# The first slice of a weight load moved from SyncE's DMA queue to ScalarE's, ahead of the edge lists

## The reference, cut to what matters

```python
h = maximum(layernorm(x), 0)                      # x: 1024 x 512, float32
q = h @ Wq + bq;  k = h @ Wk + bk;  v = h @ Wv + bv
adj = zeros(1024, 1024).at[src, dst].set(1)       # 33792 edges
a = q @ k.T / sqrt(512) * adj + (1 - adj) * (-1e6)
x = x + softmax(a) @ v
h = maximum(layernorm(x), 0)
agg = segment_sum(h[src], dst) / max(deg, 1)[:, None]
return x + h + alpha * (agg @ W.T + b)
```

## Time and profile before

| | |
|---|---|
| median of 3 runs | 245.27 us |
| the three runs | 243.74, 245.29, 245.27 us |
| the profiled execution's own time | 245.4 us |
| its span | 243.6 us |
| mean granted TensorE clock over the span | 0.993 |
| PE busy | 235.3 us (97%) |
| DVE busy | 167.7 us (69%) |
| ACT, POOL busy | 81.5 us (33%), 69.9 us (29%) |
| HBM read, written | 7.09 MB, 2.10 MB |

### The profile page before, as it was taken

How to read it: one execution, slowest core, us unless ns; L and a number is a source line. 1 busy time by engine, 2 the same in 40 slices (tenths; PEclk the granted TensorE clock), 3 DMA queues, 4 the chain that set the end, 5 groups by cost and what they waited for, 6 DMA issues and landing times.

```text
span 243.6 us, 3378 instructions
## 1 busy us (share of the span) xinstructions
PE 235.3 (97%) x1296; PEld 189.4 (78%) x1296; DVE 167.7 (69%) x348; ACT 81.5 (33%) x147; POOL 69.9 (29%) x104
## 2 busy tenths in 40 slices
PE   7999898999999996999999999999999999999995
PEld 4356687887888885888888888888888888888885
DVE  6989998999999951588457997666656254054222
ACT  2399858523322211143062425142421102050000
POOL 4155452000000005994160546162334404100000
PEclk9999999999999997999999999999999999999999
DMA  6990000000020001004000000000000000001232
GB/s 198 337 364 12 1 0 3 0 0 3 0 47 0 0 3 43 1 3 174 0 0 0 3 0 0 0 3 0 0 0 3 0 0 1 3 3 43 86 116 99
DMA packets 5617, 9.42 MB, mean 39 GB/s; under 512 B 864, under 2 KB 1376, under 8 KB 5600
## 3 DMA queue, kind: packets, MB, share of 16 engines
q1 hardware_dynamic: 4880, 8.91, 10.5%
q10 hardware_dynamic: 720, 0.28, 0.4%
HBM read 7.09 MB, written 2.10 MB: 38 GB/s over the span
## 4 chain that ended last, share of the span: by engine, by line
PE 90%; ACT 3%; DVE 2%; POOL 2%; DMA 2%; issue 1%; ACTq 0%; DVEq 0%
PE bank L799 21%; PE bank L801 20%; PE bank L800 20%; PE bank L948 12%; PE bank L820 7%; PE bank L874 3%; PE bank L968 3%; DMA src_i<-in_src 2%; PE bank L867 1%; PE bank L859 1%; POOL var_e L352 1%; POOL rstd L347 1%; ACT h L419 1%; ACT h L432 1%; ACT A L447 0%
## 5 line engine op out<-in xcount | busy, mean ns | idle before, releaser
L550 DVE TENSOR_TENSOR ohW<-iotaW,key_b 128x640 bf16<-128x640 bf16 (+4 forms) x66 | 29.8, 452 | 0.0
L546 DVE TENSOR_TENSOR ohL<-iotaL,lo_b 128x512 bf16<-128x512 bf16 x66 | 27.4, 415 | 1.8 <-PE bank L820 1.8
L799 PE MATMUL bank<-hT_hi,GT_hi 128*128 128x512 f32 x64 | 25.8, 404 | 1.9 <-DVE V_lo L642 1.9
L801 PE MATMUL bank<-hT_hi,GT_lo 128*128 128x512 f32 x64 | 25.6, 400 | 0.0
L800 PE MATMUL bank<-hT_lo,GT_hi 128*128 128x512 f32 x64 | 25.5, 399 | 0.0
L799 PE MATMUL bank<-V_hi,pT_hi 128*128 128x512 f32 x64 | 25.5, 399 | 0.0
L419 ACT ACTIVATE h2f<-xs,nmr,rstd 128x512 f32<-128x512 f32 x8 | 6.5, 817 | 56.1 <-POOL nmr L361 56.1
L800 PE MATMUL bank<-V_lo,pT_hi 128*128 128x512 f32 x64 | 24.9, 390 | 0.0
L801 PE MATMUL bank<-V_hi,pT_lo 128*128 128x512 f32 x64 | 24.9, 390 | 0.0
L948 PE MATMUL bank<-A,h_hi 128*128 128x512 f32 x64 | 24.9, 389 | 0.0
L948 PE MATMUL bank<-A,h_lo 128*128 128x512 f32 x64 | 24.9, 389 | 0.0
(11 more groups left out here) (135 smaller groups left out, 527.2 us busy)
## 6 DMA issues: line engine op xcount, KB each, us to landing
xs<-in_x SPq DMA_DIRECT2D x4, 512.0 KB, 8.8
out_dram<-o_sb SPq DMA_DIRECT2D x7, 256.0 KB, 2.0
wq_raw<-in_wqT SPq DMA_DIRECT2D x4, 256.0 KB, 6.3
wk_raw<-in_wkT SPq DMA_DIRECT2D x4, 256.0 KB, 6.9
wv_raw<-in_wv SPq DMA_DIRECT2D x1, 1024.0 KB, 12.0
wt_raw<-in_wT SPq DMA_DIRECT2D x1, 1024.0 KB, 5.4
bv_sb<-in_bv SPq DMA_DIRECT2D x1, 256.0 KB, 3.3
b_sb<-in_b SPq DMA_DIRECT2D x1, 256.0 KB, 3.2
```

Of the source, the lines that this page charges most:

```text
L546: nc.vector.tensor_tensor(ohL[:, q % RING, :, :].rearrange("p b (m two) -> p b m two", two=2), bcast(iotaL[:, :].rearrange("p (m two) -> p ...
L550: nc.vector.tensor_tensor(ohW[:, q % RING, :, 0:row].rearrange("p b (m two) -> p b m two", two=2), bcast(iotaW[:, 0:row].rearrange("p (m t ...
L799: mm(out, lhs[0][a], rhs[0][b], start=(first and k == 0), stop=False)
L801: last = mm(out, lhs[1][a], rhs[0][b], start=False, stop=(final and k == len(pairs) - 1))
```

## The change

The load of slice 0 of wk leaves SP's list, where it stood second, and becomes the first load of ACT's list, ahead of the two edge lists. Slice 0 of wq stays SP's first load. No other load, wait or operation is added or taken away; line numbers from 409 on grow by one.

```diff
-                for raw, w_d, loaded in ((wq_raw, wqT_d, ld_wq), (wk_raw, wkT_d, ld_wk)):
+                for raw, w_d, loaded in ((wq_raw, wqT_d, ld_wq), (wk_raw, wkT_d, ld_wk))[:2 if k else 1]:
                     sp.dma_start(raw[:, k, :], w_d[k * P:(k + 1) * P, :]).then_inc(loaded[k], 16)
...
         def _(act):
+            act.dma_start(wk_raw[:, 0, :], wkT_d[0:P, :]).then_inc(ld_wk[0], 16)
             act.dma_start(dst_i[:, :], dst_d).then_inc(ld_edges, 16)
             act.dma_start(src_i[:, :], src_d).then_inc(ld_edges, 16)
```

## The result

The changed kernel is slower. Its median is 248.61 us over 4 runs (248.24 to 250.08); that of the kernel before, over 4 runs, is 244.5 us (243.59 to 245.29). The ratio is 1.0181, with a 95% interval from 1.0118 to 1.0244. A second set of runs gave 1.0171 [1.0130, 1.0213], with 248.79 against 245.24. The forecast was 248.1, or +1.15% on 245.27. The mechanism that it names is in the profile; its size was too small. The time itself lies only 0.5 over the forecast, and that nearness is luck: the forecast stood on a base of 245.27, which was 244.5 here.

What follows compares the result with a forecast made beforehand. TensorE was taken as the bound, its steady work starting at `bb` behind the edge lists and VectorE's keys. 245.27 + 1.3 (late lists) + 1.6 (half clock) = 248.1 us, rounded down from 248.17; range 245.7 to 248.9.

Steps and rivals of the forecast that it cites:

- The bound and the chain: Kernel start: edge lists, VectorE's keys, then TensorE's `bb` at 9.73 set the time; later pauses move along, recovering nothing.
- Slice 0 of wk: First load on ACT's queue: lands near 4.6, starts about 4.76, ends about 8.9; gain on the path 0.
- The edge lists: ACT's queue at the start: lists queue behind wk's 144 packets, so they and `bb` come 1.3 us later.
- the 370 GB/s: DMA rate from 2.5 to 4.8 us, at which 0.54 MB ahead of the edge lists takes 1.45 us.
- The drop to 255 GB/s: Rate of the stretch with tiny packets, giving the upper bound of 2.1 us for the edge lists' delay.
- The clock: TensorE before `bb`: 2.1 us idle brings about 3.4 us at half clock between 11 and 17 us, costing 1.6 us.
- I add the differences to the median: Base of the sum: delay 1.3 and clock 1.6 are added to the earlier kernel's median of 245.27 us.
- A: At the start: edge lists late as forecast, but no clock fall in the median run; 246.6 us, chance 0.33.
- C: Pause near 93 us: its clock fall goes away in most runs, none at the start; 245.1 us, chance 0.06.
- B: ACT's queue at the start: only the issue is late, lists land 0.43 later; 245.7 us, chance 0.06.
- E: TensorE's start: `bb` would not wait for the edges, so slice 0's 0.36 us counts; 244.9 us, chance 0.03.
- D: Kernel start: lists come 2.1 us late among tiny packets, with the clock fall; 249.0 us, chance 0.05.

## Why the prediction was off

*The bound and the chain* were right: the edge lists, not the weights, set the start of `bb`, and all later pauses moved along unchanged.

*Slice 0 of wk* was right. It was issued at 0.72 and landed 3.6 us later, at 4.3 (said: 4.6), and the gain on the path was nothing. Its start at 4.49 and end near 8.1 were earlier than the 4.76 and 8.9 of the text, since TensorE reached full speed earlier in this execution (the first two weight loads of slice 0 take 0.30 us together, against 0.50 in the kernel before). So the idle time was 2.83 instead of 2.1 us.

*The edge lists* were mis-sized: +1.3 in the sum. The profile had +1.22 for `src_i` and +1.22 for `bb`, but seven profiles have +1.8 in the mean, and the runs at full clock +1.9. The division of the queues came out as read; here are the packets of the changed kernel from 2.5 to 4.8 and from 4.8 to 6 us:

```profile
DMA packets 569, 0.90 MB, mean 392 GB/s; under 512 B 63, under 2 KB 200, under 8 KB 569
q1 hardware_dynamic: 282, 0.51, 58.0%
q10 hardware_dynamic: 287, 0.39, 45.7%
...
DMA packets 273, 0.38 MB, mean 315 GB/s; under 512 B 31, under 2 KB 150, under 8 KB 273
q1 hardware_dynamic: 139, 0.25, 73.3%
q10 hardware_dynamic: 134, 0.13, 32.4%
```

The step that failed is taking the 370 GB/s for the whole way: the lists are now served across 4.8 us, where the rate falls, while before they were through at that moment. Where the rate stayed at 339 or more from 4.5 to 7 us, `src_i` was 1.2 to 1.4 later than the 5.17 of the kernel before, about as forecast; where it was 317 or less, 1.6 to 2.5. That the rate is the reason is read from these nine profiles side by side; why it falls is open. The drop to 255 GB/s stood in the earlier trace rows as an upper bound only.

By the Trainium skill, "DMA: Bandwidth & Descriptors", section "Queues, rings and completion order", the queues take turns packet by packet; 282 to 287 agrees. The same page says under "Issuing engines are not separate DMA queues" that issuing elsewhere only saves issue time. That would have made the lists 0.43 late, and no profile shows less than 1.2.

*The clock* was right in kind and place, and its price of 1.6 was right. What failed is the step "I add the differences to the median". The median of 245.27 was one of two bands, as the 243.74 among the three runs showed; I used that run to price the stretch and then took the late stretch for given on both sides. In fact the kernel before has it in 17 of 25 executions, and in 49 of 83 over the four sets of experiments. In the changed kernel all ten runs had at least one stretch and nine had two or more. So the count rose by 1.4 and not by one. With only the early pause filled, five of eight runs had one stretch, presumably the late one; that it came more often together with the early one is seen in the counts, but why was not tried. Where the third stretch of two runs lies no profile shows. Nor is the length of a pause a sure sign: behind 1.88 us in the run with `alpha` first the clock fell, behind 1.81 in the changed kernel with `alpha` late it did not, and neither behind the 2.12 that eight filling matmuls left in another.

*The rivals.* A (no fall of the clock behind the early pause) and C (fewer falls) are excluded for the median run by the clocks of the ten runs, B (only the issue is late) by every landing of `src_i`, E by the wait for `bprod`. D, which had the lists 2.1 late with the fall, 249.0, was the nearest case, and it got 0.05. In A, the idle time for lists late by 1.0 should read 1.8 us, not 1.7 (9.73 + 1.0 - 8.9).

## What to carry to other kernels

A transfer that is moved to a less busy queue goes ahead of what stood there: work out which of the two the path waits for first, and count the packets on both queues until it has landed. Where TensorE's idle time grows to about 2 us, price the half-clock stretch behind it with the delay itself, as a chance and not as a certainty; several short waits in a row can bring it as well. Read the mean clock of every run before taking a median as the base. Filling a pause with matmuls that nobody reads costs a line and gave 0.45% in the kernel before and 0.6% in the changed one. Moving a small matmul that waits behind one that does not gave some 0.3 to 0.4% at equal clock in the kernel before.

## What was not expected of the hardware

Eight idle matmuls shortened a program by 1.5 us. A load of 0.5 KB in 128 pieces at the head of a queue held up the lists behind it by 2.0 us, as much as a load of 256 KB does, and slowed the other queue too: 133 GB/s for both against 370 to 392 between 2.5 and 4.8 us. The clock fell behind a row of waits of 0.2 to 0.4 us each, with no long pause among them. And TensorE begins at its lower level without the clock's column showing it; in a profile with a wait of 2.8 us ahead of the first real matmuls their weight loads stayed 0.85 instead of 0.43 us apart up to 12.8 us.
